# GpSimd makes the remainders of q, x is loaded earlier, and all parts of two weight products become split products

## The reference, cut to what matters

```
x = x + attn(cond(x))                 # cond: x @ w_eff.T, quantized weight plus a LoRA delta
x = x + ffn(cond2(x))                 # cond2: x @ W.T + 2 * gated LoRA experts; ffn: x @ w.T + bias

cond:  delta = lora_B @ lora_A * 0.5
       cb = codebook / max(|codebook|);  scale = exp(scale_log)        # 8 levels; 16 groups of 128
       normalized = (weight + delta) / scale                           # by group
       idx = searchsorted((cb[:-1] + cb[1:]) / 2, normalized)
       w_eff = cb[idx] * scale + delta
attn:  qkv = . @ Wqkv + b; softmax(q k^T / sqrt(d)) v @ Wo + bo        # one head, d = 128
cond2: base = . @ W.T; gates: softmax of the top two of . @ Wr.T + 5 * onehot(language)
       h = . @ A.T; base + 2 * (h * gates) @ B.T
ffn:   w = s * (q - zero_point), q an integer 512x512 matrix
```

## Time and profile before

| what | value |
|---|---|
| median of 3 runs | 108.01 us (108.0 to 108.59) |
| the profiled execution: its time, its span | 107.76 us, 105.8 us |
| PE busy | 101.3 us (96%) |
| DVE busy | 67.9 us (64%) |
| ACT busy | 52.1 us (49%) |
| POOL busy | 31.8 us (30%) |
| granted PE clock | full in all 40 slices |
| loads | 9.83 MB moved, all but the stores in the first 24 us |

### The profile page before, as it was taken

One profiled execution on the slowest core, in us unless ns is written; L12 is line 12 of the kernel. 1 busy time (PEld: TensorE's weight loads), 2 busy tenths in 40 slices (PEclk: granted clock), 3 DMA queues, 4 the chain that ended last, 5 costly groups with the idle time before them and its releaser, 6 DMA issues.

```text
span 105.8 us, 1459 instructions
## 1 busy us (share of the span) xinstructions
PE 101.3 (96%) x513; PEld 84.1 (79%) x513; DVE 67.9 (64%) x163; ACT 52.1 (49%) x92; POOL 31.8 (30%) x40
## 2 busy tenths in 40 slices
PE   6999999999999999999999999999999999999980
PEld 6748568889788899899888786888898888888850
DVE  0199899889999999525999753014946802572441
ACT  4077898999989932934222239272037204002000
POOL 4000246799709570399000056400000400000000
PEclk9999999999999999999999999999999999999999
DMA  1999999960000000000000000000000640000083
GB/s 40 338 344 301 410 400 406 404 253 0 0 3 0 0 0 0 9 0 0 0 0 0 0 0 0 6 0 0 0 0 0 237 160 0 6 0 0 3 297 99
DMA packets 4599, 9.83 MB, mean 93 GB/s; under 512 B 752, under 2 KB 1008, under 8 KB 4592
## 3 DMA queue, kind: packets, MB, share of 16 engines
q1 hardware_dynamic: 4448, 9.48, 24.6%
q10 hardware_dynamic: 144, 0.26, 0.6%
HBM read 7.64 MB, written 2.10 MB: 92 GB/s over the span
## 4 chain that ended last, share of the span: by engine, by line
PE 89%; DMA 4%; DVE 2%; ACT 1%; DVEq 1%; issue 0%
PE psum L860 19%; PE psum L862 19%; PE psum L861 19%; PE psum L885 7%; DMA lora<-in_lora 4%; PE psum L876 3%; PE psum L895 3%; PE psum L910 3%; PE psum L901 3%; PE psum L905 3%; PE psum L1010 2%; PE psum L1031 2%; PE psum L1025 2%; ACT moe L462 1%; PE psum L1017 1%; PE psum L926 1%
## 5 line engine op out<-in xcount | busy, mean ns | idle before, releaser
L662 DVE COPY_PREDICATED cond_work<-cond_work,psum 128x1024 f32<-128x1024 int32 x10 | 13.7, 1366 | 1.1 <-ACT cond_work L363 0.7
L860 PE MATMUL psum<-G_hi,xT_hi 128*128 128x512 f32 x32 | 12.7, 398 | 0.0
L862 PE MATMUL psum<-G_hi,xT_lo 128*128 128x512 f32 x32 | 12.5, 390 | 0.0
L861 PE MATMUL psum<-G_lo,xT_hi 128*128 128x512 f32 x32 | 12.5, 390 | 0.0
L363 ACT ACTIVATE cond_work<-cond_n,cut_bias 128x1024 f32<-128x1024 f32 x10 | 11.2, 1143 | 0.6 <-DVE cond_n L699 0.6
L578 POOL TENSOR_TENSOR hl<-hl,hl_bias 128x272 f32<-128x272 f32 (+2 forms) x4 | 3.1, 774 | 26.4 <-ACT hl L374 14.4
L523 POOL TENSOR_TENSOR xT_lo<-xT,xT_hi 128x1024 fp32r<-128x1024 f32 x4 | 9.6, 2411 | 3.2 <-DVE cond_work L668 3.2
L860 PE MATMUL psum<-xT_hi,split_b_hi 128*128 128x512 f32 x24 | 9.6, 401 | 0.0
L862 PE MATMUL psum<-xT_hi,split_b_lo 128*128 128x512 f32 x24 | 9.4, 391 | 0.0
L861 PE MATMUL psum<-xT_lo,split_b_hi 128*128 128x512 f32 x24 | 9.4, 390 | 0.0
L885 PE MATMUL psum<-hlT,xT 128*128 128x136 f32 x64 | 8.4, 281 | 0.0
(11 more groups left out here) (166 smaller groups left out, 237.4 us busy)
## 6 DMA issues: line engine op xcount, KB each, us to landing
out<-cond_work SPq DMA_DIRECT2D x7, 256.0 KB, 2.1
cond_n<-in_cond_w SPq DMA_DIRECT2D x2, 512.0 KB, 6.6
xT<-in_x_t SPq DMA_DIRECT2D x2, 512.0 KB, 7.6
q_i<-in_q_t SPq DMA_DIRECT2D x4, 256.0 KB, 7.4
...
```

Source lines behind the costliest of these rows:

```text
L662: dve.copy_predicated(half(level, h), beyond[n % len(beyond)].bitcast(I32), psum[EARLY][:, j + 1:j + 2].to_broadcast([P, 2 * C])).then_inc ...
L860: pe.matmul(out_ap, l_hi, r_hi, start=first, stop=False)
L861: pe.matmul(out_ap, l_hi, r_lo, start=False, stop=False)
L862: return pe.matmul(out_ap, l_lo, r_hi, start=False, stop=last)
```

## The change: what it does, and the diff

Loads (SP): x's first pair stands behind hlT, before the first half of the cond weight; the second half of the cond weight goes behind all parts of q and moe. No load is added or taken away.

TensorE: the four blank products behind the LoRA product are gone. Part 0 of `G` and of `Bf` are split products too. The LoRA product writes to banks 0, 1, 4 and 5, so `x_hl(0)` goes to bank 6. In parts 1 to 3 of `G` the product with moe's remainder comes before that with q's remainder.

GpSimd now makes q's remainders for parts 1 to 3 (`w_rest`, VectorE did), moe's remainder for part 0, the lowest level of half 0 (ScalarE did), expb's remainder with 512 columns (before 384), and w_eff's remainders 0 and 1 (VectorE did). The waits without data are gone.

VectorE: `levels` are multiplied by the groups' scales once (112 numbers into PSUM, 16 into `floor`), so `pick` copies scaled levels, by group of 128 columns, and `w_eff` is one addition of 512 columns (before four of 128 with multiplication). It makes q's remainder of part 0 early.

The core of the diff:

```diff
             load("small", small[:, :], small_in)
-            load("cond_w0", cond_n[:, 0:2, :], cond_w[:, 0:2, :])
             load("hlT", hlT[:, :, :], hl_t)
             load("x0", xT[:, 0, :, :], x_t[0])
             load_proj_weights(0)
+            load("cond_w0", cond_n[:, 0:2, :], cond_w[:, 0:2, :])
             load_proj_weights(1)
-            load("cond_w1", cond_n[:, 2:4, :], cond_w[:, 2:4, :])
             load_proj_weights(2)
             load_proj_weights(3)
+            load("cond_w1", cond_n[:, 2:4, :], cond_w[:, 2:4, :])
 ...
             delta_out(0)
             delta_out(1)
-            set_level()
             delta_out(2)
             delta_out(3)
-            beyond_cut(0, 0)
-            beyond_cut(1, 0)
+            w_hi(0)
+            moe_hi(0)
             moe_hi(1)
             w_hi(1)
-            beyond_cut(2, 0)
-            hl_raw(0, 4)
+            beyond_cut(0, 0)
+            w_hi(2)
             moe_hi(2)
-            w_hi(2)
-            beyond_cut(3, 0)
+            beyond_cut(1, 0)
             moe_hi(3)
             w_hi(3)
+            beyond_cut(2, 0)
+            hl_raw(0, 6)
+            beyond_cut(3, 0)
             beyond_cut(4, 0)
             x_hi(0)
             beyond_cut(5, 0)
             act.wait_ge(loaded["exp_b"], 16)
-            rounded(expb_hi[:, 1:CT, :], expb[:, 1:CT, :], expb_hi_ready)
+            rounded(expb_hi[:, :, :], expb[:, :, :], expb_hi_ready)
 ...
+            def w_eff_rest(o):
+                pool.wait_ge(w_eff_hi_ready, o + 1)
+                rest(split_a_lo[:, o, :], level[:, o, :], split_a_hi[:, o, :], w_eff_lo_ready)
+
+            def w_rest(o):
+                pool.wait_ge(w_hi_ready, o + 1)
+                rest(split_b_lo[:, o, :], w_ffn[:, o, :], split_b_hi[:, o, :], w_lo_late_ready)
 ...
-            moe_rest(1)
-            moe_rest(2)
-            pool.wait_ge(picked, 3)
-            moe_rest(3)
-            pool.wait_ge(w_lo_ready, 3)
+            pool.wait_ge(floor_ready, 1)
+            pool.tensor_copy(by_group(half(level, 0)), floor_of(0)).then_inc(level_set, 1)
+            moe_rest(0)
+            for o in range(1, CT):
+                moe_rest(o)
+                w_rest(o)
 ...
             pool.wait_ge(expb_hi_ready, 1)
-            rest(expb_lo[:, 1:CT, :], expb[:, 1:CT, :], expb_hi[:, 1:CT, :], expb_lo_ready)
+            rest(expb_lo[:, :, :], expb[:, :, :], expb_hi[:, :, :], expb_lo_ready)
             x_lo(0)
-            pool.wait_ge(w_eff_ready, 2)
             x_lo(1)
+            w_eff_rest(0)
             wqkv_rest(0)
-            pool.wait_ge(w_eff_lo_ready, 2)
+            w_eff_rest(1)
             wqkv_rest(1)
 ...
-                dve.copy_predicated(half(level, h), beyond[n % len(beyond)].bitcast(I32),
-                                    psum[EARLY][:, j + 1:j + 2].to_broadcast([P, 2 * C])).then_inc(picked, 1)
+                at = GROUPS * j + GROUPS // 2 * h
+                dve.copy_predicated(by_group(half(level, h)), by_group(beyond[n % len(beyond)].bitcast(I32)),
+                                    psum[EARLY][:, at:at + GROUPS // 2].unsqueeze(2).to_broadcast(
+                                        [P, GROUPS // 2, P])).then_inc(picked, 1)
 ...
-                for g in range(CT * o, CT * (o + 1)):
-                    ins = dve.scalar_tensor_tensor(g_block(level, g), g_block(level, g), scale[:, g:g + 1],
-                                                   g_block(delta, g), ALU.mult, ALU.add)
-                ins.then_inc(w_eff_ready, 1)
+                dve.tensor_tensor(level[:, o, :], level[:, o, :], delta[:, o, :], ALU.add).then_inc(w_eff_ready, 1)
 ...
+            w_full(0)
+            w_lo(0)
             w_delta_first()
+            w_full(1)
             dve.wait_ge(wd_ready, 1)
             dve.wait_ge(inv_scale_ready, 1)
             dve.tensor_tensor(blocks(0), blocks(0), inv_scale[:, 0:GROUPS // 2].unsqueeze(2).to_broadcast(
                 [P, GROUPS // 2, P]), ALU.mult).then_inc(norm_first_ready, 1)
-            w_full(0)
+            w_full(2)
             pick(0, 0)
-            w_full(1)
-            pick(1, 0)
-            w_lo(1)
-            w_full(2)
-            pick(2, 0)
-            w_lo(2)
             w_full(3)
-            pick(3, 0)
-            w_lo(3)
+            for j in range(1, 4):
+                pick(j, 0)
 ...
-            idle_turns(FILL)
 ...
-            x_hl(0, 4)
-            G_first()
+            x_hl(0, 6)
+            G_product(0)
             G_product(1)
 ...
-            pe.matmul(psum[4][:, :], expb[:, 0, :], w_ffn[:, 0, :], start=True, stop=False)
             pe.wait_ge(expb_lo_ready, 1)
-            for o in range(1, CT):
+            for o in range(CT):
                 mm = three(psum[4][:, :], expb_hi[:, o, :], expb_lo[:, o, :], split_b_hi[:, o, :],
-                           split_b_lo[:, o, :], False, o == CT - 1)
+                           split_b_lo[:, o, :], o == 0, o == CT - 1)
```

More of the change, by code:

```diff
@@ L346, in w_hi @@
                 rounded(split_b_hi[:, o, :], w_ffn[:, o, :], w_hi_ready)
-            def set_level():
-                act.wait_ge(ones_ready, 1)
-                act.wait_ge(levels_ready, 1)
-                act.activation(half(level, 0), ones[:, 0:1].to_broadcast([P, 2 * C]), ACT.Identity,
-                               bias=levels[:, 0:1], scale=0.0).then_inc(level_set, 1)
             def beyond_cut(j, h):
@@ L555, in _ @@
                 [P, GROUPS // 2, P]), ALU.mult).then_inc(norm_late_ready, 1)
-            pool.tensor_copy(half(level, 1), levels[:, 0:1].to_broadcast([P, 2 * C])).then_inc(level_late_set, 1)
+            pool.tensor_copy(by_group(half(level, 1)), floor_of(1)).then_inc(level_late_set, 1)
             pool.wait_ge(expb_hi_ready, 1)
-            rest(expb_lo[:, 1:CT, :], expb[:, 1:CT, :], expb_hi[:, 1:CT, :], expb_lo_ready)
+            rest(expb_lo[:, :, :], expb[:, :, :], expb_hi[:, :, :], expb_lo_ready)
             x_lo(0)
-            pool.wait_ge(w_eff_ready, 2)
             x_lo(1)
+            w_eff_rest(0)
             wqkv_rest(0)
-            pool.wait_ge(w_eff_lo_ready, 2)
+            w_eff_rest(1)
             wqkv_rest(1)
@@ L566, in _ @@
             wqkv_rest(3)
-            pool.wait_ge(w_eff_lo_ready, CT)
+            pool.wait_ge(w_eff_late_lo_ready, 2)
             pool.wait_ge(woT_hi_ready, 1)
@@ L875, in _ @@
             for o in range(CT):
-                pe.matmul(psum[o][:, :], lora[:, 0, o * P:(o + 1) * P], lora[:, 1, :], start=True, stop=True)\
+                pe.matmul(psum[DELTA_BANKS[o]][:, :], lora[:, 0, o * P:(o + 1) * P], lora[:, 1, :], start=True, stop=True)\
                   .then_inc(delta_done, 1)
-            idle_turns(FILL)
             def x_hl(part, bank, batches=None, base=0):
```

72 lines of the change are left out of this document (42 added, 30 removed).

## The result

The changed kernel takes **111.88 us** (median of four executions: 110.58, 111.45, 112.32, 114.48), against 108.0 for the kernel before, run beside it; ratio **1.0285, interval 1.0222 to 1.0347**, slower. Forecast: 112.4, range 108.6 to 113.6. The profiled execution took 111.45, with a span of 109.5: +3.7 on before.

The account below looks back on a forecast made before the run. GpSimd's list was taken as the new bound, swallowing TensorE's saved 1.97 us. With VectorE and GpSimd blocking each other, +1.9 us by the first meeting and +2.5 by the second make +4.4: 112.4 us, range 108.6 to 113.6.

Parts of the forecast that it names:

- the first meeting: GpSimd's early remainders and VectorE's addition and division block each other, delaying the first cut: y_x(1) starts +1.9 us.
- GpSimd's list as the new bound: Even with nothing blocked, GpSimd has expb's remainder ready only at 27.5; TensorE waits, y_x(0) late by about 0.5 us.
- rival 2: No blocking that counts between VectorE and GpSimd: +0.5 us, median 108.5 (107.8 to 109.0); chance 0.14.
- TensorE's own 1.97 us: Saved on TensorE: blank products 1.06, part 0 of G 0.73, Bf 0.18; all lost to GpSimd's queue.
- The block between VectorE and GpSimd: A VectorE instruction with two large SBUF inputs and a GpSimd one exclude each other; the blocked one ends 0.12 to 0.16 early.
- Loads: With the cond weight's half behind them, x's pair, q's and moe's part 0 land 1.3 to 1.4 us earlier.
- The second meeting: x_lo(1) on GpSimd takes the ports between w_eff(0) and w_eff(1); Bf's remainder comes late, y_x(0) starts at 37.0, not 34.5.
- rival 1: w_eff(1) keeps the ports behind w_eff(0): y_x(0) +1.9 us, median 109.9 (109.2 to 110.8); chance 0.27.
- rival 5: Reordered loads don't land earlier, moe's part 0 stays at 10.5: +5.4 us, or +2.9; chance 0.09 together with another rival.
- Edits costed at nothing: GpSimd's level copy, w_eff as one addition, and picks and copy by group: taken as 0 us on the path.

Follow-up runs that it names:

- e5: Changed kernel with one old wait put back: GpSimd's x_lo(1) waits until both w_eff additions are done; 111.93 us, ratio 1.0375.
- e8: Changed kernel unaltered, run again beside e5; 112.47 us, ratio 1.0431.
- e9: Changed kernel with the wait of e5 and the loads in the order of the kernel before; 111.88 us, ratio 1.0386.
- e1: Changed kernel, but VectorE's addition of the LoRA delta, division and conversions of q read one operand from PSUM; 110.41 us, ratio 1.021.
- e6: Changed kernel with the edits of e1 and e5 together; 110.00 us, ratio 1.0191.
- e7: Changed kernel with only q's conversions reading their factor from PSUM, without the wait of e5; 111.83 us, ratio 1.0348.
- e3: Changed kernel, but VectorE makes q's remainders of parts 1 to 3 again; 117.79 us, ratio 1.0931.
- e11: Kernel of e6 with expb's rounding on ScalarE and its remainder on GpSimd moved ahead; 110.32 us, ratio 1.0243.
- e4: Kernel before, without GpSimd's four waits for results it doesn't read; 112.48 us, ratio 1.0388.
- e2: Changed kernel, but ScalarE rounds x's second pair one cut earlier, so x_lo(1) asks before w_eff(0); 113.59 us, ratio 1.0521.
- e10: Kernel before with only the scaled levels: picks by group, w_eff one addition per part; 108.45 us, ratio 1.0029.

## Why the prediction was right or wrong

**One measure for all runs.** q's first part lands earlier or later by execution, and the rest follows it. From the start of its conversion to the start of Bf it takes 30.42 - 8.90 = 21.52 us in the changed kernel, 21.51 in e5 (10.12 to 31.63), 21.54 in e8 (9.76 to 31.30), 21.52 in e9 (9.83 to 31.35). With no block it is 19.20 in e1 and 19.22 in e6 (9.74 to 28.96), with the conversions alone free 20.69 in e7 (9.28 to 29.97). So **the first meeting costs 2.3 us, and 0.83 of them come from the conversions' part in it**.

**GpSimd's list as the new bound: right.** With q at 8.5 the forecast had the remainder of expb ready at 27.5 if nothing is blocked, 19.0 behind the conversion; e6 has 19.22 to Bf's start. TensorE waits there in every run of the change but e3 and e11. What failed in the case with nothing blocked (rival 2, +0.5, 108.5) is where the list starts: e6 took 2.2 more than the kernel before, and y_x(0) is 1.90 late in it. Of the 1.4 beyond the forecast's 0.5, 1.24 are q, converted at 9.74 and not at 8.5, and 0.2 the conversions, 0.75 with an operand in PSUM instead of 0.55.

**TensorE's own 1.97 us, given back before they reach the end: right.** TensorE reaches Bf at 29.33 and finds nothing to do; even unblocked (e6) it waits 1.07 there, and y_x(1) is 1.91 later than before. Two sizes were off without effect. `x_hl` starts 0.75 earlier (8.45 for 9.20), not 1.06, and Bf takes 2.82 for 2.92, 0.10 less and not 0.18; the forecast had TensorE at Bf "at about 25", but it had already waited inside G, 1.58 before part 1 alone.

**The block between VectorE and GpSimd: right as a mechanism.** e1 takes it away by an operand in PSUM, e4 brings it into the kernel before. The instruction that waits ends 0.14 to 0.15 earlier than its own full time after the release (addition 1.08 for 1.22; w_eff 0.54 for 0.69), as in the rows before; for the conversion it is 0.27 (0.28 for 0.55). The Trainium skill (SBUF — State Buffer, A bandwidth-pool intuition that's wrong) has a DMA, whose descriptors GpSimd must write, blocked until 0.115 us behind the end of VectorE's instruction. The prediction took this figure for any blocked instruction; in these traces the blocked ones end less than their own length behind the release.

**The first meeting: mis-sized.** "+1.9" was 3.38. The step that failed is that q's conversions pass beside GpSimd's remainders: that of part 1 in 0.45 ("conversion to 13.1"), those of parts 2 and 3 without a cost. That of part 1 took 1.50; this hardly moved the first cut, for the division behind it found the ports free. Counted from the conversion of part 0, the cut starts after 6.78 in the changed kernel and 6.64 in e7. The conversion of part 2 took 1.52; ScalarE's roundings of part 2, and GpSimd's remainder behind them, came 0.55 later than in e7 (9.46 and 8.91). The conversion of part 3 held the ports against that remainder, 0.29 more. Together that is the 0.83 that e7 gives back.

The forecast allowed the lock only to an instruction "with two large inputs in SBUF", because the only blocked rows before were of that kind. From the conversion's start to y_x(1) the forecast had 31.8 - 8.5 = 23.3; e7, where the conversions are free, has 32.79 - 9.28 = 23.51, and the changed kernel 33.24 - 8.90 = 24.34. The Trainium skill (SBUF — State Buffer, SBUF: two separate sides) also names an instruction "in a 2-port perf mode" as a holder of the lock. The conversion, 512 columns in 0.55 where a two-input instruction takes 0.69, may be one; that it is locked is shown (1.50 and 1.52, two more in e3), why is not, since e7 changed the operation together with the place of its factor.

**Loads: wrong.** "1.3 to 1.4 us earlier" was 0.9 for q in the profiled execution (8.90 against 9.8 in e9), and nothing in e8 (9.76) and e5 (10.12). This is 0.4 of the first meeting's error of 1.4 in the profiled execution; 0.8 are the conversions, and 0.2 stay open. Moe's part 1, which was to stay at 11.9, landed at 12.2 in the changed kernel and 13.1 in e8. The byte count took one rate for the whole stretch: between 6.0 and 7.5 us the loads of the changed kernel moved 188 to 209 GB/s, those of the kernel before 399 to 418, whose slow stretch (147 to 172) lay between 8.0 and 9.0. What sets the slow stretch wasn't tested.

**The second meeting: the mechanism exists, its outcome is not fixed.** The forecast put +2.5 on it with x_lo(1) winning. In the profiled execution w_eff(1) kept the ports (rival 1), and the pair took 1.30. In e7 and e1 x_lo(1) won, and y_x(0) waited 1.98 and 2.07; in e2 it asked first, and y_x(0) waited 1.04. e6 removes it from e1. Of the ten executions of the changed kernel two were profiled (111.45 and 112.28), both with the short form; 114.48 may have had the long one.

**Why the time was right all the same: luck.** Forecast +1.9 and +2.5; measured +3.4 and 0. Two errors of opposite sign, 1.5 and 2.5, and 0.3 behind y_x(0) that the forecast did not have. What happened in the profiled execution is rival 1, whose 109.9 (109.2 to 110.8) the conversions and the loads left too low; rival 5, loads that don't land earlier, had +2.9 with it.

**Edits costed at nothing: right.** Picks by group take 1.33 to 1.40, before 1.34 to 1.39, and e10 shows no change by the scaled levels alone (interval 0.9994 to 1.0065).
